# Row gathers of a graph-attention layer, spaced on GpSimd's queue instead of tied to the stages of the score expansion

## The reference

```python
h = (x @ W).reshape(n, 8, 32)
a_src = einsum('nhc,hc->nh', h, att_src); a_dst = einsum('nhc,hc->nh', h, att_dst)
e = leaky_relu(a_src[src] + a_dst[dst], 0.2)          # one score per edge and head
m = segment_max(e, dst); e = exp(e - m[dst])
out = segment_sum(h[src] * alpha[:, :, None], dst)    # alpha = e / sum of e by dst
```

## Time and profile before

| what | us |
|---|---|
| median of 3 runs | 2971.29 (2961.16 to 2977.59) |
| profiled execution, span | 2974.2 |
| expansion with its gathers | 2186 to 2536 |
| merge | 2565 to 2903 |
| TensorE / VectorE / GpSimd busy | 2470.6 / 1396.0 / 936.7 |

### The profile page before, as it was taken

The page is one execution under the profiler, slowest core; times in us unless marked ns, Lnnn a source line. Parts: engine busy times, 40 slices in busy tenths (PEclk is TensorE's granted clock), DMA queues, the critical chain, the costliest instruction groups (busy, mean ns, idle before and its releaser), DMA issues. The chain is left out here.

```text
span 2974.2 us, 32381 instructions
## 1 busy us (share of the span) xinstructions
PE 2470.6 (83%) x9483; PEld 1621.2 (55%) x9484; DVE 1396.0 (47%) x3940; ACT 707.2 (24%) x1552; POOL 936.7 (31%) x927
## 2 busy tenths in 40 slices
PE   3677789897987999999999999999977886457680
PEld 2444788343766555565556555577743444345560
DVE  7999656455665001030101001455575664546668
ACT  3776545111443000010001000255400000103112
POOL 0000256666666000000000000012167666576740
PEclk9888999998998999999999999999988998678885
DMA  6565678343344743444444434333558887646641
GB/s 233 243 253 225 212 238 264 118 138 97 112 121 137 152 151 129 151 134 151 129 152 133 151 119 145 93 106 102 113 168 271 278 282 245 209 132 190 192 127 43
DMA packets 209534, 493.89 MB, mean 166 GB/s; under 512 B 46457, under 2 KB 128430, under 8 KB 209134
## 3 DMA queue, kind: packets, MB, share of 16 engines
q1 hardware_dynamic: 135185, 301.30, 32.2%
q10 hardware_dynamic: 38173, 133.27, 12.8%
q0 software_dynamic: 36032, 57.60, 7.1%
HBM read 374.71 MB, written 117.32 MB: 165 GB/s over the span
## 5 line engine op out<-in xcount | busy, mean ns | idle before, releaser
L794 POOL DMA_INDIRECT table_dense_weights<-pair_weight,dst x416 | 411.2, 988 | 563.5 <-DVE weights_c L849 324.8
L1526 PE MATMUL banks<-own_term,features_and_rows 128*128 128x391 f32 (+1 forms) x1656 | 552.3, 491 | 0.0
L2134 POOL DMA_INDIRECT features_and_rows<-table_heads,src x376 | 401.7, 1068 | 191.4 <-issue 107.9
L1526 PEld LDWEIGHTS banks<-own_term,features_and_rows 128*128 128x128 f32 x1656 | 312.2, 189 | 226.8
L1552 DVE TENSOR_SCALAR features_and_rows<-banks,hop_bias 128x391 f32<-128x391 f32 (+1 forms) x24 | 15.0, 625 | 762.2 <-PE banks L1526 762.2
L954 PE MATMUL banks<-split_rows,count_columns 128*128 128x512 f32 x1200 | 322.1, 415 | 19.6 <-issue 12.6
L2531 PE MATMUL banks<-features_and_rows,edge_to_window 128*128 x880 | 233.4, 427 | 104.5 <-DVE edge_to_window L2492 71.6
L1526 PE MATMUL banks<-features_and_rows 128*128 128x391 f32 (+1 forms) x840 | 282.4, 491 | 0.0
L954 PEld LDWEIGHTS banks<-split_rows,count_columns 128*128 128x128 f32 x1200 | 226.3, 193 | 76.8 <-issue 21.7
L2531 PEld LDWEIGHTS banks<-features_and_rows,edge_to_window 128*128 128x128 f32 x880 | 181.3, 210 | 156.5 <-issue 122.5
L558 PE MATMUL banks<-features_and_rows,pair_and_bias_rows 128*128 128x400 f16 x806 | 184.3, 388 | 87.1 <-DVE features_and_rows L540 51.9
(11 more groups left out here) (425 smaller groups left out, 3016.8 us busy)
## 6 DMA issues: line engine op xcount, KB each, us to landing
hidden<-table_counts SPq DMA_DIRECT2D x305, 160.0 KB
table_dense_weights<-weights_c ACTq DMA_DIRECT2D x26, 1600.0 KB, 5.7
own_term<-table_dense_weights SPq DMA_DIRECT2D x52, 782.0 KB
features_and_rows<-table_rows_by_edge SPq DMA_DIRECT2D x58, 528.0 KB
own_term<-table_dense_weights SPq DMA_DIRECT2D x34, 780.5 KB
pair_and_bias_rows<-table_edge_rows ACTq DMA_DIRECT2D x50, 512.0 KB
weights_c<-table_edge_rows ACTq DMA_DIRECT2D x50, 512.0 KB
table_rows_by_edge<-features_and_rows SPq DMA_DIRECT2D x48, 528.0 KB
```

What stands on the lines that cost most here:

```text
L794: e.indirect_dma_start(out=self.table, out_offset=bass.IndirectOffsetOnAxis(ap=self.place[:, t:t + 1], axis=0), in_=self.values[:, t:t + 1 ...
L1526: m = e.matmul(psum[b][:, 0:wide], z_block(block)[:, f * P:(f + 1) * P], streamed[tile % STREAM][:, lo - from_column:lo - from_column + wi ...
L2134: e.indirect_dma_start(out=to[:, k, :], out_offset=None, in_=t_h, in_offset=bass.IndirectOffsetOnAxis(ap=src[:, t:t + 1], axis=0)).then_in ...
```

## The change

The wait on `s_masked` in `gather_group` is removed, with its constant and parameter. Behind each of the 416 row gathers and each of the 25 gathers of the segment maximum GpSimd now runs a counter operation of 128 columns into a buffer that nobody reads, which waits for the one before it. The waits on a number in a register get a register AND with 511 ahead of them instead of a register copy (403 in `build_pe`, about 200 in `build_act`, some 24 in the second layer, 25 in `merge_act`), and a remainder by 32 in `merge_pe` becomes an AND with 31.

```diff
+PAUSE = 128
+        spare_count = sb("spare_count", [P, PAUSE], I32)
+        def wait_loaded(e, sem, loaded, bound):
+            e.reg_alu(bound, loaded, 511, ALU.bitwise_and)
+            e.wait_ge(sem, bound)
+
+        s_paused, paused = pr.sem("pause_done"), [0]
+
+        def pause(e):
+            if paused[0]:
+                e.wait_ge(s_paused, paused[0])
+            e.iota(spare_count[:, :], [[1, PAUSE]], base=0, channel_multiplier=0).then_inc(s_paused, 1)
+            paused[0] += 1
...
-                e.wait_ge(s_zeroed, e.snap(regs[2 * n + 1], min_val=3, max_val=WINDOWS + 2))
+                wait_loaded(e, s_zeroed, regs[2 * n + 1], bound)
...
-                e.wait_ge(s_built, e.snap(regs[v % ROTATING], min_val=1, max_val=BUILD_STEPS))
+                wait_loaded(e, s_built, regs[v % ROTATING], bound)
...
-                        e.wait_ge(weights.steps, e.snap(reg, min_val=1, max_val=STEPS))
+                        wait_loaded(e, weights.steps, reg, stream_register[1])
...
-        STAGES_BEHIND = 3
...
-        def gather_group(e, quad, to, sem, stage=0):
+        def gather_group(e, quad, to, sem):
             for k in range(GROUP):
                 t = quad * GROUP + k
-                if k % 2 == 0 and stage + k // 2 > 0:
-                    e.wait_ge(s_masked, stage + k // 2)
                 e.indirect_dma_start(out=to[:, k, :], out_offset=None, in_=t_h,
                                      in_offset=bass.IndirectOffsetOnAxis(ap=src[:, t:t + 1], axis=0)).then_inc(sem, 16)
+                pause(e)
...
-                gather_group(e, STAGED_QUADS[n], staging[d], s_staged[d], GROUP // 2 * n - STAGES_BEHIND)
+                gather_group(e, STAGED_QUADS[n], staging[d], s_staged[d])
...
             for j in range(NODE_TILES):
                 e.indirect_dma_start(out=mx[:, j, :], out_offset=None, in_=t_run,
                                      in_offset=bass.IndirectOffsetOnAxis(ap=last_at[:, j:j + 1], axis=0)).then_inc(s_last, 16)
+                pause(e)
...
-                    e.wait_ge(s_begun, step % 32)
+                    e.wait_ge(s_begun, step & 31)
...
-                e.wait_ge(s_mm, e.snap(ends_of_node[d], min_val=1, max_val=MERGE_STEPS + UNROLL))
+                wait_loaded(e, s_mm, ends_of_node[d], bound)
```

More of the change, by code:

```diff
@@ L547, in build_pe @@
             pe_regs.extend(e.alloc_register(f"step_{k}") for k in range(2 * REGS_AT_ONCE))
-            regs = pe_regs
+            regs, bound = pe_regs, e.alloc_register("zeroed_windows")
             for s in range(BUILD_STEPS):
@@ L565, in build_act @@
             regs = [e.alloc_register(f"window_end_{k}") for k in range(ROTATING)]
+            bound = e.alloc_register("window_end_step")
             for b in [RUN_BANK, RUN_BANK + 1, *range(ROTATING)]:
@@ L1619, in hops_sp @@
                     e.wait_ge(*ready)
-                stream_register.append(e.alloc_register("weight_steps_in_memory"))
+                stream_register.extend((e.alloc_register("weight_steps_in_memory"), e.alloc_register("weight_steps_awaited")))
             reg = stream_register[0]
@@ L2537, in merge_act @@
             ends_of_node = [e.alloc_register(f"node_end{k}") for k in range(NODE_TILES)]
+            bound = e.alloc_register("node_end_step")
             e.load(ends_of_node, merge_control[0:1, MERGE_STEPS:MERGE_STEPS + NODE_TILES])
```

## The result

The changed kernel takes **3032.43 us** (median of 4 runs, 3027.41 to 3036.34), the kernel before, run beside it, 2972.08 (4 runs, 2961.16 to 2977.59): ratio 1.0207, 95% interval 1.018 to 1.0234. It is about 2% slower, outside the range of the forecast (2912 to 3018 us) and on the other side. The profiled execution has a span of 3034.5 us.

A forecast was written before the change was run, and what follows sets the result against it. GpSimd's queue was taken as the bound: 686.4 - 80.2 of waits + 70.6 of pauses = 676.8 us, last gather at 2863.3, end 2954.5; less 2.9 from profile to median, 2952 us predicted, range 2912 to 3018.

The forecast's parts named there:

- step 4: Expansion and merge: gaps between gathers let TensorE's increments pass, so all 80.2 us of GpSimd's true waits go.
- Step 1: Staged gathers in the expansion: removing the wait for masks before every second gather frees 28 us of the 80.2.
- Step 2: GpSimd's gathers: 441 added pauses cost 0.16 us each, 70.6 us in all, with nothing hiding them.
- GpSimd as the bound: From expansion to merge: GpSimd has little slack, needing 606.2 of 686.4 us without waits, and its last gathers release the end.
- Steps 3 and 5: Gathers stretched by VectorE's operations stay as they are; register ANDs in build and merge cost 0.
- The last lag: End of the merge: 11.9 us from the last gather's end to the last scaling shrink to 1.8.
- The second: Rival: stalls have another cause, or a 0.46 us gap does not let them pass; 2996 us, chance 0.10.
- c: Added time per pause between two gathers on GpSimd, put at 0.16 us, with bounds of 0.05 and 0.53.
- The dear pause: Rival: the counter also waits for the gather's after-work, 0.31 us added per pause; 3018 us, chance 0.20.
- the wait at the staging buffers: Rival in the expansion: without mask waits gathers run into the write-back; a few us at most, inside the middle case.

The follow-up runs named there:

- neither: Changed kernel without its pauses, so no mask waits and no counters: 3140.3 and 3194.5 us in two runs on chip E, 2803.17 us on chip B.
- experiment 8: Changed kernel with counters of one column instead of 128, chip D: 2811.66 us, ratio 1.003 to the kernel before.
- experiment 5: Changed kernel with three counters instead of one behind each of the 416 row gathers, chip C: 3087.32 us, ratio 1.1011 to the kernel before.
- experiments 10 and 11: Changed kernel on chip E: with three counters behind each staged gather and none elsewhere, 3104.69 us; without any pauses, 3140.3 and 3194.5 us.
- experiment 9: Changed kernel without pauses, its 232 staged gathers replaced by plain copies of consecutive table rows on SP's queue, chip C: 2764.19 us, ratio 0.9858.

## Why the prediction was wrong

**What failed is step 4, "What the gaps give back".** It let the whole 80.2 us of waits vanish, because a gather every 1.41 us would let TensorE's increments pass. The waits came to 89.0 us. The step rested on one stretch of 10 us with 7 gathers 1.4 us apart in which nothing was late. GpSimd in order of time in that stretch, kernel before:

```profile
2648.39 0.94 POOL L2134 DMA_INDIRECT features_and_rows<-table_heads,src  x1 [0.30 <-issue]
2649.63 1.69 POOL L2134 DMA_INDIRECT features_and_rows<-table_heads,src  x1 [0.30 <-issue]
2651.63 0.94 POOL L2134 DMA_INDIRECT features_and_rows<-table_heads,src  x1 [0.30 <-PE banks L2531]
2652.88 2.01 POOL L2134 DMA_INDIRECT features_and_rows<-table_heads,src  x1 [0.31 <-issue]
```

The mean distance was 1.4 us because some gathers took 1.7 to 2.0 us; the gaps were the plain 0.30. The stretch said nothing about a longer gap, and it shows that gathers at the plain gap don't hold TensorE up all the time either. With a gap of 0.42, 2360 to 2388 has 20 gathers 1.38 us apart and TensorE busy a third of the time. A gap of 0.42 helps a little and not enough. On chip E the distance can be followed: 299.7, 242.0 and 65.2 us of idle time before the masks at gaps of 0.305, 0.42 and about 1.02 us.

**Step 1 has the wrong sign, and this is where the loss comes from.** The removed waits were booked as 28 us of GpSimd time that comes back. On a held chip they are what keeps the expansion moving: a late mask stops the gathers, in the stop the increments come through (the two at 2288.9 above), and the stages catch up. Taking the conditions away costs 157 us on E (2983.2 to 3140.3, and 211 by the other run of neither); the pauses then win back 71 (3069.2; 125 by the other run), though they are 52 us of work themselves. So on E the two edits have opposite signs, +157 and -71, and together make +86; on A only the sum of the two was measured, +60. From first mask to last the expansion takes 341 us before on A, 412 changed on A, 443 changed and 498 with neither on E. On a free chip the conditions are worth 0 and the pauses cost 47 to 49. That the changed kernel loses on all three chips on which it ran (2.1% on A, 1.7% on C, 2.9% on E) hides two different reasons.

**Step 2, the price of a pause**, was right in kind and mis-sized: 0.117 us instead of 0.16, 52 us instead of 70.6. The seam ahead of the counter is 0.01 and not 0.08, and its 128 columns take 0.25 and not 0.23. With the true price and the rest of the forecast the sum would be 2933 us: the error of this term went against that of step 4.

**GpSimd as the bound** is right on the free chips: what is added to its queue shows up at the end, from 10 us (experiment 8) to 285 (experiment 5). On the held ones the queue alone doesn't set the time: with neither edit it has the least to do and the kernel takes longest.

**Steps 3 and 5** held. The stretch changed by 3.3 us, the register edits gave a ratio of 0.9993.

**The last lag** of 11.9 us, of which 10 were to vanish, is 11.0. The increments of the merge's matmuls are late as well: of 440, 335 are recorded, 22 of them over 1 us after the latest matmuls that were over, 48 of 347 before, and none in the traces of free chips.

**The rivals.** The second, by its clause that the gap does not let the releases pass, was the true one and had a tenth of the chances. It gave 2996 us, since it kept the waits as they were and still removed the conditions for nothing. With c = 0.117 it would have given 2977. The missing 55 us go with the expansion's growth, which neither the forecast nor this rival had: the last mask is at 2600.9 instead of 2532.4. How much of these 68 us GpSimd's slack absorbs was not measured by itself. Its other clause, a cause that has nothing to do with gathers, is refuted by experiments 10 and 11, where on one chip the spacing of the gathers alone takes the late increments away. The Trainium skill (SBUF — State Buffer, Who interferes with whom) says that TensorE never waits on anyone at the SBUF. The traces agree, since TensorE starts within 0.15 us of what it needs on held chips too; that section speaks of access to that memory and not of the increments that were late here, so it did not bear on this rival. The dear pause (c = 0.31) is refuted by 0.117, the wait at the staging buffers by 6.0 us, 5.8 before.

**What stays open.** Why A and E delay TensorE's increments while GpSimd issues indirect DMAs close behind each other, and the other four do not. Two more things differ in the traces of the held chips and are not explained: records of increments are missing, VectorE's among them, and the count matrix's scatters take 80 us longer. Whether the gathers or the writes back beside them hold the increments up was not parted, as experiment 9 ran on a free chip. Whether single gaps of 1 us would be enough, and whether conditions with pauses would beat the kernel before on a held chip, was not seen there. The split +157 and -71 rests on one set of runs on E, with two runs of neither 54 us apart; its signs are the same by either of them.

## What to carry to other kernels

A wait that looks like lost time in one engine's account can be the valve of another's: before taking it out, look at what starts moving when it stops the queue (here TensorE's late increments), and book that on the other side of the sum. A gap in a busy queue is paid for at its full price times its count, so price the seam from both neighbours (0.01 behind a gather, 0.16 ahead of one), and before trusting one stretch of 10 us, look at its single instructions and at other stretches like it: here the gaps that it seemed to be about had not changed. And when a trace shows a delay that no instruction explains, run the unchanged kernel on a second chip first: here 144 us of idle time before the masks on one chip were 59 on the next, with only the register edits between them.

## What the hardware showed that was not expected

- On A and E increments that TensorE's matmuls raise arrive late while GpSimd starts an indirect DMA every 1.25 us: a mask starts up to 39.9 us after the six matmuls that it needs. With 1.98 us between starts no mask of 112 is late. TensorE's waits for VectorE in the expansion were never late (at most 0.15 us), on any chip.
- The unchanged kernel takes 2972 to 2983 us on these and 2802 to 2805 on three others, 6% apart (F: 2799 to 2808).
- The 0.305 us between two indirect DMAs shrink to 0.16 ahead of one that follows a counter, and a counter starts 0.01 us behind one; so a counter of one column (0.143 us) fits into the gap (0.311 in all), while the gathers take 962 ns in the median with it instead of 946.
